# A cross-attention and FFN kernel: VectorE takes head 0's scores first, the next queries move ahead of the attention in odd heads, and the last scores get two empty banks

## The chip, the core and the metric

The kernel runs on one core of a Trainium2 chip. The metric is the device time of one launch in microseconds (us), as the median of several runs. The inputs lie in the device's memory, the output is written back to it, and nothing else is counted.

## The reference: what is computed

`x` has 8 sequences of 128 rows of 512 elements, `ctx` the same shape. The layer is a layer norm, an RMS norm, cross attention with 32 heads of width 128, a residual sum, a second layer norm and a product with a 512 x 512 matrix that is decoded from 4-bit codes (plus a low-rank term that the kernel folds into that matrix).

```python
def xattn(hidden, kv, mask, position_bias, ln_weight, w_q, w_k, w_v, w_out):
    x = rmsnorm(hidden, ln_weight)
    h_q = (x @ w_q.T).reshape(b, lq, H, DH)          # H = 32, DH = 128
    h_k = (kv @ w_k.T).reshape(b, lk, H, DH)
    h_v = (kv @ w_v.T).reshape(b, lk, H, DH)
    score = einsum('bqhd,bkhd->bhqk', h_q, h_k) + position_bias[None]
    score = softmax(where(mask, score, -inf))
    attn = einsum('bhqk,bkhd->bqhd', score, h_v).reshape(b, lq, H * DH)
    return hidden + attn @ w_out.T

x = x + xattn(layernorm(x), ctx_4096, mask, ...)
x = x + ffn(layernorm(x), w_codes, absmax, W_a, W_b)  # x @ W.T + 2 * (x @ W_a @ W_b)
```

## The kernel before

**Tiling.** All 8 sequences are taken together as 1024 columns, in two halves of 512 (`hf` 0 and 1, four sequences each). A 32-bit matmul of full precision is slow, so each operand is held as a high part (`..._hi`, rounded by ScalarE) and a low part (`..._lo`, the remainder, from VectorE or GpSimd), and `three` (L1176) issues three matmuls for each pair of tiles: high by high, low by high, high by low. `scores` (L1212) and `attend` (L1218) work on plain 32-bit tiles.

**Loops.** Heads go in groups of four (`g`), within a group `j` = 1 to 4 (head `h = 4 g + j`); head 0 is done in the prologue, and head 31 in an epilogue. Each engine has its own instruction stream, written out by hand, and the streams meet only in semaphores: `x.wait_ge(sem, n)`. So the order in each stream is the order of the calls in the source. Seven groups run in a loop, the eighth (heads 29 and 30, then 31) is written behind it.

**Keys in pairs.** The keys of two heads are made together from seven products, `key_product(m, 0..6)` of 6 matmuls each, which share three PSUM banks (w_ps0, w_ps1, w_ps2). Products 0, 2, 3 and 6 all accumulate in w_ps0. What stands there after product 0, and again after product 2, is a result of its own, and ScalarE copies it out (`copy_keys(m, n)`, L604, `kT<-w_ps`): copy 0 after product 0, copy 1 after product 1, copy 2 after product 2, copy 3 after product 6. Hence TensorE waits for copy 0 ahead of product 2 and for copy 2 ahead of product 3 (`pe.wait_ge(keys_copied, COPIES * m + 3)`).

**An odd head on TensorE** (h = 1, 3, ..., 29; `odd_head`), in this order: scores of head h; key products 0 and 1; attention of head h-1 (`attend`, which reads the probabilities pT); key product 2; the first half of the next head's queries (`queries(h + 1, 0, ...)`, 12 matmuls in a bank of its own, o_ps0); key products 3 and 4; the second half of the queries; key products 5 and 6.

**The softmax of head h.** VectorE adds the bias to the scores (L990, `p<-s_ps,p`) and takes the maxima (L992); ScalarE takes the exponentials with their sums (L653, 8 instructions) and then normalises (L604, `p_blocks<-p_blocks,row_scale`, 8 instructions), for which VectorE makes the factors (L997, L999); VectorE turns 32 x 32 blocks (L1007), and 16 DMAs of the SP queue (L341) move the blocks across partitions into pT. ScalarE's exponentials of head h+1 write p_blocks again, so they wait for these DMAs (`pT_loaded`). GpSimd writes the next head's bias into `p` (`make_bias`, L497) when the exponentials are done, splits key weights (L469, `ring_lo`), forms their sums (L459), and decodes the FFN weights in between (L532, L535).

**ScalarE in an odd head:** exponentials of the first half; copy 0; exponentials of the second half; 8 normalisations; copies 1 and 2; key weights 4, 5 and 6 (`ring_hi<-k_raw`); the two halves of the attention (`attn_hi<-s_ps`); queries (`qT<-o_ps`), weights, and so on.

**The prologue on VectorE**, behind the split of the normalised input: `residual(b)` for b = 0 to 3 (L942: `resid` scaled and shifted in place, which nothing reads before the first output sum), a context split (L893, `ctx_lo`), `residual(b)` for b = 4 to 7, the last context split (`split_first(7)`), the low part of head 1's query weights (`split_q(1)`, `q_lo`), and only then head 0's bias and maxima.

Of the kernel before, what the change touches and what calls it, by code (L numbers as in the profile page):

```python
# [7 lines left out]
B = 8  # L8
# [3 lines left out]
H = 32  # L12
# [6 lines left out]
HB = B // 2  # L19
# [42 lines left out]
SPLITS = 8  # L62
# [24 lines left out]
def key_slot(j, p):  # L87

    return (p + (PRODUCTS if j == 3 else 0)) % RING
# [6 lines left out]
def xattn_ffn(nc, x_d, ctx_d, mask_d, lnw_d, q_d, k_d, pos_d, wo_d, wv_d, codes_d, absmax_d, wa_d, wb_d, out_d):  # L96
    lora_d = nc.dram_tensor("lora_dram", (GROUPS, P, SLICE), f32, kind="Internal").ap()
    ffn_d = nc.dram_tensor("ffn_dram", (GROUPS, P, SLICE), f32, kind="Internal").ap()
    with ExitStack() as ctx:
# [107 lines left out]
            return s_ps[i][:, :, :].rearrange("p b k -> p (b k)")  # L207


        last_s = [s_ps[0][:, :, :], w_ps[2][:, :].rearrange("p (b k) -> p b k", b=HB)]  # L210

        tile_ps = [o_ps[0][:, :], o_ps[1][:, :], o_ps[2][:, :], w_ps[2][:, :]]

# [100 lines left out]
        def _(sp):  # L314
            def load_q(h):
                sp.dma_start(q_raw[:, :], q_d[h]).then_inc(q_loaded, 16)
# [50 lines left out]
            sp.wait_ge(mask_done, 2)  # L367
            load_codes(0)

            sp.wait_ge(ctx_lo_done, SPLITS)  # L370
            load_wo(0, 0)
            load_wo(1, 1)

# [8 lines left out]
            move_blocks((2, 3))  # L382
            sp.wait_ge(q_lo_done, 3)
            load_q(3)

            def group(g, last):
                for j in range(1, G if last else G + 1):
# [214 lines left out]
        def _(act):  # L602
# [167 lines left out]
            act.wait_ge(lora_stored, 16 * C)  # L770
            copy_first_values(6)
            copy_first_values(7)
            for p_at in range(2):
                split_k(1, p_at, key_slot(1, p_at))
            drain_q(1, 0, next_queries[0])
            for p_at in (2, 3):
                split_k(1, p_at, key_slot(1, p_at))
            drain_q(1, 1, next_queries[1])
            split_q(2)

            def odd_head(g, j, last):
# [109 lines left out]
        def _(dve):  # L891
# [176 lines left out]
            for b in range(HB):  # L1068
                residual(b)
            split_first(6, ctx_lo[:, 2, :, :], ctx_sum[1], ctx_hi[:, 2, :, :])  # L1070
            for b in range(HB, B):
                residual(b)
            split_first(7, ctx_lo[:, 4, :, :], ctx_sum[3], ctx_hi[:, 4, :, :])
            split_q(1)


            for hf in range(2):
                bias_and_max(0, hf)
            for hf in range(2):
                scale_rows(0, hf)  # L1080
            turn_blocks(0)
            split_q(2)

            def odd_head(g, j, last):
# [84 lines left out]
        def _(pe):  # L1169
# [149 lines left out]
            def odd_head(g, j, last):  # L1319

                h = G * g + j
                m = 2 * g + (j + 1) // 2

                pe.wait_ge(keys_added, ADDS * m)
                pe.wait_ge(attn_lo_done, 2 * (h - 1) + 2)
                scores(h, 0)

                if j == 1:
                    pe.wait_ge(values_copied, 2 * COPIES * (g + 1))
                key_product(m, 0, key_slot(j, 0))  # L1330
                key_product(m, 1, key_slot(j, 1))
                if j == 1:
                    pe.wait_ge(values_added, 2 * ADDS * (g + 1))
                pe.wait_ge(pT_loaded, 16 * NQ * NQ * h)
                for hf in range(2):
                    pe.wait_ge(biased, 2 * h + hf + 1)
                    attend(j - 1, hf, s_flat(hf), moved)
                pe.wait_ge(keys_copied, COPIES * m + 1)
                key_product(m, 2, key_slot(j, 2))

                if j == 3:
                    pe.wait_ge(out_added, B * (2 * g + 1))
                queries(h + 1, 0, query_bank(j, 0))
                pe.wait_ge(keys_copied, COPIES * m + 3)
                key_product(m, 3, key_slot(j, 3))
                key_product(m, 4, key_slot(j, 4))
                queries(h + 1, 1, query_bank(j, 1))
                key_product(m, 5, key_slot(j, 5))
                pe.wait_ge(keys_added, ADDS * m + 1)
                key_product(m, 6, key_slot(j, 6))  # L1350
# [50 lines left out]
            even_head(GROUPS - 1, 2, True)  # L1401


            pe.wait_ge(attn_lo_done, 2 * (H - 2) + 1)
            pe.wait_ge(keys_added, ADDS * PAIRS)
            scores(H - 1, 0, last_s)
            pe.wait_ge(wo_lo_done, H - 2)
            for b in range(B):
                if b % HB == 0:
                    pe.wait_ge(attn_lo_done, 2 * (H - 2) + 1 + b // HB)  # L1410
                if b in TURN_BEFORE:
# [2 lines left out]
                    for i, at in enumerate(halves(hf)):  # L1414
                        t = pe.transpose(s_ps[hf][:, i, :], p[:, at, :], ident[:, :])
                    t.then_inc(turned, 1)
                if b == 3:

                    pe.wait_ge(biased, 2 * (H - 1) + 2)
                if b >= 4:  # L1420
                    pe.wait_ge(out_added, B * (PAIRS - 2) + b - 3)
                output(b, wo_hi, wo_lo)
# [71 lines left out]
```

## Time and profile before

| | |
|---|---|
| median of 3 runs | 841.38 us (840.92 to 841.69) |
| the profiled execution's own time | 841.95 us |
| its span from the first to the last instruction | 840.1 us |
| TensorE busy | 826.6 us of the span |
| one group of four heads in the loop | 97.28 us |
| mean granted TensorE clock | 0.996 of full speed |

The execution that was profiled took 0.57 us longer than the median, and 1.85 us of its time lie outside the span. Times in rows are us from the start of the span.

### The profile page before, as it was taken

What the parts mean: (1) busy time and instruction counts of PE and PEld (TensorE: products, weight loads), DVE (VectorE), ACT (ScalarE), POOL (GpSimd) and SP (SyncE); (2) the same over time, 40 slices, a digit from 0 to 9 for tenths busy, and PEclk for the clock granted to TensorE, in tenths of its full rate; (3) what the DMA queues carried; (4) which work ended last, traced back from release to release, by engine and by line L of the source; (5) the groups of instructions that cost most, each with busy time, mean ns of one, the idle gap of its engine ahead of it and who ended that gap; (6) DMA issues with size and microseconds to landing.
All of it is one profiled execution on the core that took longest, in us unless ns stands there. A gap on an engine that the chain in (4) does not pass through costs nothing.

```text
span 840.1 us, 15757 instructions
## 1 busy us (share of the span) xinstructions
PE 826.6 (98%) x4694; PEld 721.4 (86%) x4694; DVE 450.4 (54%) x754; ACT 445.8 (53%) x1297; POOL 537.5 (64%) x556
## 2 busy tenths in 40 slices
PE   9997999999999999999999999999999999999998
PEld 6876888988889888998889888898889888898786
DVE  6783656246553556246562565436562455626683
ACT  5746555364644656264644557446553546437632
POOL 1654778756784668757786577756687567865440
PEclk9998999999999999999999999999999999999999
DMA  8213323123221223113231133112230232311102
GB/s 327 83 42 94 96 71 98 27 68 109 85 69 53 91 66 95 33 62 96 69 97 60 47 110 97 37 53 92 68 97 28 67 97 69 105 42 51 45 13 88
DMA packets 51125, 64.98 MB, mean 77 GB/s; under 512 B 11008, under 2 KB 37248, under 8 KB 50080
## 3 DMA queue, kind: packets, MB, share of 16 engines
q1 hardware_dynamic: 51104, 64.73, 24.7%
q8 instruction: 10, 0.16, 0.1%
q14 instruction: 11, 0.09, 0.0%
HBM read 44.24 MB, written 4.19 MB: 58 GB/s over the span
## 4 chain that ended last, share of the span: by engine, by line
PE 86%; DVE 5%; ACT 4%; SPq 3%; DMA 1%; issue 1%; POOL 0%; ACTq 0%; POOLq 0%; DVEq 0%
PE w_ps L1176 41%; PE o_ps L1176 32%; PE s_ps L1212 6%; PE s_ps L1218 6%; SPq L341 3%; ACT p_blocks L653 2%; ACT p_blocks L604 1%; DVE ctx_lo L893 1%; DMA pT<-p_blocks 1%; DVE stats L899 1%; DVE resid L1015 1%; DVE resid L942 1%; DVE xn_lo L948 1%; PE s_ps L1242 0%; DVE wv_raw L966 0%
## 5 line engine op out<-in xcount | busy, mean ns | idle before, releaser
L497 POOL TENSOR_TENSOR p<-pos_raw,mask_add 128x1024 f32<-128x1024 f32 x32 | 69.6, 2175 | 113.7 <-ACT p_blocks L653 113.5
L532 POOL TENSOR_SCALAR picked<-codes 128x256 f32<-128x256 int32 x112 | 125.4, 1120 | 19.2 <-POOL level L535 15.6
L653 ACT ACTIVATE p_blocks<-p,neg_max 128x128 f32<-128x128 f32 x248 | 96.1, 389 | 57.1 <-DVE neg_max L992 46.5
L535 POOL TENSOR_TENSOR level<-level,picked 128x256 f32<-128x256 f32 x112 | 89.9, 803 | 20.8 <-POOL picked L532 20.8
L469 POOL TENSOR_TENSOR ring_lo<-k_raw,ring_hi 128x256 fp32r<-128x256 f32 x105 | 76.9, 744 | 30.2 <-ACT ring_hi L604 27.2
L604 ACT ACTIVATE ring_hi<-k_raw 128x256 fp32r<-128x256 f32 x105 | 38.7, 412 | 103.3 <-POOL k_raw L459 103.3
L1015 DVE TENSOR_TENSOR resid<-o_ps,resid 128x512 f32<-128x512 f32 x102 | 68.7, 686 | 44.5 <-PE o_ps L1176 44.3
L1176 PE MATMUL w_ps<-ctx_hi,ring_hi 128*128 128x512 f32 x210 | 85.2, 406 | 0.5 <-ACT kT L604 0.5
L1176 PE MATMUL w_ps<-ctx_hi,ring_lo 128*128 128x512 f32 x210 | 82.4, 392 | 0.0
L1176 PE MATMUL w_ps<-ctx_lo,ring_hi 128*128 128x512 f32 x210 | 82.2, 392 | 0.0
L604 ACT ACTIVATE p_blocks<-p_blocks,row_scale 128x128 f32<-128x128 f32 x248 | 77.1, 390 | 1.1 <-DVE row_scale L999 1.1
L1212 PEld LDWEIGHTS s_ps<-kT,qT 128*128 128x128 f32 x504 | 62.1, 195 | 10.0 <-ACT qT L604 6.4
L1176 PE MATMUL o_ps<-wo_hi,attn_hi 128*128 128x512 f32 x180 | 70.3, 391 | 0.3 <-DVE attn_lo L893 0.3
L1212 PE MATMUL s_ps<-kT,qT 128*128 128x128 f32 x504 | 63.5, 280 | 7.1 <-ACT qT L604 7.1
L1176 PE MATMUL o_ps<-wo_hi,attn_lo 128*128 128x512 f32 x180 | 70.1, 389 | 0.0
L1176 PE MATMUL o_ps<-wo_lo,attn_hi 128*128 128x512 f32 x180 | 70.0, 389 | 0.0
L990 DVE TENSOR_TENSOR p<-s_ps,p 128x512 f32<-128x512 f32 x63 | 43.2, 686 | 40.9 <-PE s_ps L1212 40.9
L1007 DVE STREAM_TRANSPOSE p_blocks<-p_blocks 128x512 f32<-128x512 f32 x62 | 40.5, 691 | 38.0 <-ACT p_blocks L604 38.0
L1218 PEld LDWEIGHTS s_ps<-pT,v 128*128 128x128 f32 x480 | 58.2, 191 | 2.3
L1218 PE MATMUL s_ps<-pT,v 128*128 128x128 f32 x480 | 58.4, 275 | 0.0
L893 DVE TENSOR_TENSOR attn_lo<-s_ps,attn_hi 128x512 fp32r<-128x512 f32 x62 | 40.9, 680 | 31.1 <-ACT attn_hi L604 31.1
L982 DVE TENSOR_TENSOR v<-w_ps,v 128x512 f32<-128x512 f32 x21 | 14.5, 692 | 76.6 <-PE w_ps L1176 76.6
(223 smaller groups left out, 2287.9 us busy)
## 6 DMA issues: line engine op xcount, KB each, us to landing
pT<-p_blocks SPq DMA_DIRECT2D x496, 32.0 KB, 1.8
k_raw<-k_dram SPq DMA_DIRECT2D x16, 512.0 KB, 3.3
wv_raw<-wv_dram SPq DMA_DIRECT2D x8, 1024.0 KB, 4.9
q_raw<-q_dram SPq DMA_DIRECT2D x32, 256.0 KB, 3.5
wo_raw<-wo_dram SPq DMA_DIRECT2D x32, 256.0 KB, 3.9
resid<-x_dram SPq DMA_DIRECT2D x2, 1024.0 KB, 12.0
pos_raw<-pos_dram SPq DMA_DIRECT2D x32, 64.0 KB, 3.9
out_dram<-resid SPq DMA_DIRECT2D x8, 256.0 KB, 2.0
```

The costliest lines, as they stand in the source:

```text
L469: return pool.tensor_tensor(out, whole, hi.bitcast(f32), ALU.subtract)
L497: pool.tensor_tensor(p[:, :, :], pos, mask_add[:, :, :], ALU.add).then_inc(bias_done, 1)
L532: then(pool.tensor_scalar((level if code == 0 else picked)[:, :], codes[:, :], float(code), NF4[code], match, ALU.mult))
L535: then(pool.tensor_tensor(level[:, :], level[:, :], picked[:, :], ALU.add))
L604: return act.activation(out, in_, ACT.Copy, **kw)
L653: e = act.activation(out(b), p[:, b, :].rearrange("p (k c) -> p k c", c=Q), ACT.Exp, bias=neg_max[:, b:b + 1], accum_out=prob_sum[:, b:b + 1])
L893: return dve.tensor_tensor(out, whole, hi.bitcast(f32), ALU.subtract)
L990: dve.tensor_tensor(p[:, bs, :], banks[hf][:, :, :], p[:, bs, :], ALU.add).then_inc(biased, 1)
L1015: dve.tensor_tensor(resid[:, b, :], bank, resid[:, b, :], ALU.add).then_inc(out_added, 1)
L1176: mm = pe.matmul(out, l, r, start=opens and i == 0, stop=closes and i == n - 1, skip_group_check=True)
L1212: s = pe.matmul(banks[hf][:, i, :], qT[:, at], kT[:, slot, at], start=True, stop=True)
L1218: o = pe.matmul(out[:, i * L:(i + 1) * L], v[:, b, j * DH:(j + 1) * DH], by_keys(b), start=True, stop=True)
```

## The change

It has four parts, and no instruction is added or taken away.

1. VectorE's prologue: head 0's bias and maxima stand right behind the split of context part 6. `split_q(1)` follows, then the factors of half 0, `residual(4)`, the factors of half 1, `residual(5)` to `residual(7)`, the turn of the blocks, and last `split_first(7)`. SP waits for five context splits, no longer for all eight, ahead of its first output-weight loads; the wait for all eight stands further down.
2. ScalarE's prologue: the copies of head 1's queries (`drain_q(1, 0)`, `drain_q(1, 1)`) stand behind the first and the second key weight split, no longer behind the second and the fourth.
3. TensorE's odd heads: `queries(h + 1, 0, ...)` stands behind key product 1, ahead of the attention, no longer between key products 2 and 3. Its wait for the output sums moves with it.
4. The epilogue: the scores of head 31 go to the banks o_ps2 and w_ps2, no longer s_ps0 and w_ps2; the wait for the attention's low part goes, and output 2 waits for the first half's bias sum.

```diff
-        last_s = [s_ps[0][:, :, :], w_ps[2][:, :].rearrange("p (b k) -> p b k", b=HB)]
+        last_s = [bank[:, :].rearrange("p (b k) -> p b k", b=HB) for bank in (o_ps[2], w_ps[2])]
@@ sync
-            sp.wait_ge(ctx_lo_done, SPLITS)
+            sp.wait_ge(ctx_lo_done, 5)
             load_wo(0, 0)
             load_wo(1, 1)
...
             load_q(3)
+
+            sp.wait_ge(ctx_lo_done, SPLITS)
@@ scalar
-            for p_at in range(2):
-                split_k(1, p_at, key_slot(1, p_at))
+            split_k(1, 0, key_slot(1, 0))
             drain_q(1, 0, next_queries[0])
+            split_k(1, 1, key_slot(1, 1))
+            drain_q(1, 1, next_queries[1])
             for p_at in (2, 3):
                 split_k(1, p_at, key_slot(1, p_at))
-            drain_q(1, 1, next_queries[1])
             split_q(2)
@@ vector
             split_first(6, ctx_lo[:, 2, :, :], ctx_sum[1], ctx_hi[:, 2, :, :])
-            for b in range(HB, B):
-                residual(b)
-            split_first(7, ctx_lo[:, 4, :, :], ctx_sum[3], ctx_hi[:, 4, :, :])
-            split_q(1)
             for hf in range(2):
                 bias_and_max(0, hf)
-            for hf in range(2):
-                scale_rows(0, hf)
+            split_q(1)
+            scale_rows(0, 0)
+            residual(HB)
+            scale_rows(0, 1)
+            for b in range(HB + 1, B):
+                residual(b)
             turn_blocks(0)
+            split_first(7, ctx_lo[:, 4, :, :], ctx_sum[3], ctx_hi[:, 4, :, :])
             split_q(2)
@@ tensor, odd_head
                 key_product(m, 1, key_slot(j, 1))
                 if j == 1:
                     pe.wait_ge(values_added, 2 * ADDS * (g + 1))
+                else:
+                    pe.wait_ge(out_added, B * (2 * g + 1))
+                queries(h + 1, 0, query_bank(j, 0))
                 pe.wait_ge(pT_loaded, 16 * NQ * NQ * h)
                 for hf in range(2):
                     pe.wait_ge(biased, 2 * h + hf + 1)
                     attend(j - 1, hf, s_flat(hf), moved)
                 pe.wait_ge(keys_copied, COPIES * m + 1)
                 key_product(m, 2, key_slot(j, 2))
-
-                if j == 3:
-                    pe.wait_ge(out_added, B * (2 * g + 1))
-                queries(h + 1, 0, query_bank(j, 0))
                 pe.wait_ge(keys_copied, COPIES * m + 3)
                 key_product(m, 3, key_slot(j, 3))
@@ tensor, epilogue
-            pe.wait_ge(attn_lo_done, 2 * (H - 2) + 1)
             pe.wait_ge(keys_added, ADDS * PAIRS)
             scores(H - 1, 0, last_s)
...
-                if b == 3:
-                    pe.wait_ge(biased, 2 * (H - 1) + 2)
+                if b in (2, 3):
+                    pe.wait_ge(biased, 2 * (H - 1) + b - 1)
```

TensorE's stream in an odd head of the loop, from the attention (`s_ps<-pT,v`) on, before. The six `w_ps<-ctx...` rows are key product 2, `o_ps<-xn_hi,q_hi` is the first matmul of the next queries, and ISA and REGISTER_ALU rows carry waits and counters.

```order
L1218 MATMUL s_ps<-pT,v 128x128 x8
L1338 ISA
L1182 REGISTER_ALU
L1176 MATMUL w_ps<-ctx_hi,ring_hi 128x512
L1176 MATMUL w_ps<-ctx_lo,ring_hi 128x512
L1176 MATMUL w_ps<-ctx_hi,ring_lo 128x512
L1176 MATMUL w_ps<-ctx_hi,ring_hi 128x512
L1176 MATMUL w_ps<-ctx_lo,ring_hi 128x512
L1176 MATMUL w_ps<-ctx_hi,ring_lo 128x512
L1202 REGISTER_ALU
L1176 MATMUL o_ps<-xn_hi,q_hi 128x512
```

The same place in the change, again from the attention on:

```order
L1221 MATMUL s_ps<-pT,v 128x128 x8
L1345 ISA
L1185 REGISTER_ALU
L1179 MATMUL w_ps<-ctx_hi,ring_hi 128x512
L1179 MATMUL w_ps<-ctx_lo,ring_hi 128x512
L1179 MATMUL w_ps<-ctx_hi,ring_lo 128x512
L1179 MATMUL w_ps<-ctx_hi,ring_hi 128x512
L1179 MATMUL w_ps<-ctx_lo,ring_hi 128x512
L1179 MATMUL w_ps<-ctx_hi,ring_lo 128x512
L1347 REGISTER_ALU
L1185 REGISTER_ALU
L1179 MATMUL w_ps<-ctx_hi,ring_hi 128x512
```

The queries stood behind key product 2; now L1347, the wait for the copy, and key product 3 stand right behind it.

VectorE's stream in the prologue before, from context split 6 on (`p<-s_ps,p` and `neg_max` are head 0's bias and maxima, `recip` and `row_scale` its factors):

```order
L893 TENSOR_TENSOR ctx_lo<-wv_raw,ctx_hi 128x1024
L942 TENSOR_SCALAR resid<-resid,ln_scale,ln_shift 128x512 x4
L893 TENSOR_TENSOR ctx_lo<-wv_raw,ctx_hi 128x1024
L893 TENSOR_TENSOR q_lo<-q_raw,q_hi 128x512
L990 TENSOR_TENSOR p<-s_ps,p 128x512
L992 TENSOR_REDUCE neg_max<-p 128x4
L990 TENSOR_TENSOR p<-s_ps,p 128x512
L992 TENSOR_REDUCE neg_max<-p 128x4
L997 RECIPROCAL recip<-prob_sum 128x4
L999 TENSOR_TENSOR row_scale<-recip,row_valid 128x4
L997 RECIPROCAL recip<-prob_sum 128x4
L999 TENSOR_TENSOR row_scale<-recip,row_valid 128x4
```

And in the change, from the same split on:

```order
L895 TENSOR_TENSOR ctx_lo<-wv_raw,ctx_hi 128x1024
L992 TENSOR_TENSOR p<-s_ps,p 128x512
L994 TENSOR_REDUCE neg_max<-p 128x4
L992 TENSOR_TENSOR p<-s_ps,p 128x512
L994 TENSOR_REDUCE neg_max<-p 128x4
L895 TENSOR_TENSOR q_lo<-q_raw,q_hi 128x512
L999 RECIPROCAL recip<-prob_sum 128x4
L1001 TENSOR_TENSOR row_scale<-recip,row_valid 128x4
L944 TENSOR_SCALAR resid<-resid,ln_scale,ln_shift 128x512
L999 RECIPROCAL recip<-prob_sum 128x4
L1001 TENSOR_TENSOR row_scale<-recip,row_valid 128x4
L944 TENSOR_SCALAR resid<-resid,ln_scale,ln_shift 128x512 x3
```

Four residuals and one context split stood ahead of the bias sum. Now one residual stands between the factors and three stand between the last factor and the turn of the blocks.

## Rows read from the trace of the kernel before

**Rows 1.** The page, part 1: busy us (share of span) xinstructions.

```profile
PE 826.6 (98%) x4694; PEld 721.4 (86%) x4694; DVE 450.4 (54%) x754; ACT 445.8 (53%) x1297; POOL 537.5 (64%) x556
```

**Rows 2.** TensorE's waits: us in total, times, longest us.

```profile
PE s_ps L1212 <- ACT qT L604: 7.1, 3, 4.8
...
PE w_ps L1176 <- ACT kT L604: 0.5, 1, 0.5
```

**Rows 3.** Stretch of one group: us, then busy us of each engine, clock, DMA.

```profile
245.33:342.61 97.28, 97.28 (x574) 86.25 (x573) 49.62 (x84) 51.58 (x157) 67.69 (x69) 1.00 0.24 73
```

**Rows 4.** Timeline of TensorE in odd head 13: start us, us, instruction.

```profile
368.52 1.95 PE L1218 MATMUL s_ps<-pT,v 128*128 128x128 f32 x16
370.22 0.48 PE L1176 MATMUL w_ps<-ctx_hi,ring_hi 128*128 128x512 f32 x1
...
371.46 0.39 PE L1176 MATMUL w_ps<-ctx_hi,ring_lo 128*128 128x512 f32 x1
371.69 0.40 PE L1176 MATMUL o_ps<-xn_hi,q_hi 128*128 128x512 f32 x1
...
374.43 0.39 PE L1176 MATMUL w_ps<-ctx_hi,ring_hi 128*128 128x512 f32 x1
...
379.64 0.39 PE L1176 MATMUL o_ps<-xn_hi,q_lo 128*128 128x512 f32 x1
```

**Rows 5.** Timeline of ScalarE in the same head.

```profile
372.59 1.06 ACT L604 ACTIVATE kT<-w_ps 128x512 f32<-128x512 f32 x2
373.55 1.02 ACT L604 ACTIVATE ring_hi<-k_raw 128x256 fp32r<-128x256 f32 x3
...
380.07 0.60 ACT L604 ACTIVATE qT<-o_ps 128x512 f32<-128x512 f32 x1 [3.01 <-PE o_ps L1176]
```

**Rows 6.** Timeline of GpSimd in the same head.

```profile
374.13 2.14 POOL L469 TENSOR_TENSOR ring_lo<-k_raw,ring_hi 128x256 fp32r<-128x256 f32 x3 [1.29 <-ACT ring_hi L604]
```

**Rows 7.** Timeline of TensorE, head 0's scores to head 1.

```profile
49.03 2.01 PE L1212 MATMUL s_ps<-kT,qT 128*128 128x128 f32 x16
...
66.71 1.88 PE L1212 MATMUL s_ps<-kT,qT 128*128 128x128 f32 x8 [4.76 <-ACT qT L604]
...
81.87 0.49 PE L1176 MATMUL w_ps<-ctx_hi,ring_hi 128*128 128x512 f32 x1 [0.48 <-ACT kT L604]
```

**Rows 8.** Timeline of VectorE in the prologue.

```profile
46.02 2.58 DVE L942 TENSOR_SCALAR resid<-resid,ln_scale,ln_shift 128x512 f32<-128x512 f32 x4
...
49.66 3.13 DVE L942 TENSOR_SCALAR resid<-resid,ln_scale,ln_shift 128x512 f32<-128x512 f32 x4
...
54.45 0.68 DVE L990 TENSOR_TENSOR p<-s_ps,p 128x512 f32<-128x512 f32 x1
...
59.33 2.00 DVE L999 TENSOR_TENSOR row_scale<-recip,row_valid 128x4 f32<-128x4 f32 x1
62.67 1.30 DVE L1007 STREAM_TRANSPOSE p_blocks<-p_blocks 128x512 f32<-128x512 f32 x2 [1.34 <-ACT p_blocks L604]
```

**Rows 9.** Timeline of ScalarE: head 0's normalisation, head 1's exponentials, copies 1 and 2.

```profile
58.99 1.27 ACT L604 ACTIVATE p_blocks<-p_blocks,row_scale 128x128 f32<-128x128 f32 x4
...
74.76 0.40 ACT L653 ACTIVATE p_blocks<-p,neg_max 128x128 f32<-128x128 f32 x1 [4.79 <-DMA pT<-p_blocks]
...
80.68 1.05 ACT L604 ACTIVATE kT<-w_ps 128x512 f32<-128x512 f32 x2
```

**Rows 10.** Timelines of GpSimd and of SP's queue: head 1's bias, head 0's moves.

```profile
59.16 2.15 POOL L497 TENSOR_TENSOR p<-pos_raw,mask_add 128x1024 f32<-128x1024 f32 x1 [6.65 <-ACT p_blocks L653]
...
63.41 10.08 SPq L341 DMA_DIRECT2D pT<-p_blocks  x16
```

**Rows 11.** Timelines of ScalarE and TensorE ahead of head 31's scores.

```profile
781.60 1.06 ACT L604 ACTIVATE qT<-w_ps 128x512 f32<-128x512 f32 x2
...
782.32 1.13 PE L1212 MATMUL s_ps<-kT,qT 128*128 128x128 f32 x8 [1.37 <-ACT qT L604]
```

**Rows 12.** Stretch behind TensorE's long pause, columns as in rows 3.

```profile
67.00:71.00 4.00, 3.07 (x15) 2.78 (x15) 0.99 (x2) 1.72 (x4) 3.02 (x5) 0.50 0.20 52
```

## The prediction

> **What bounds the kernel now.** I read the busy times first: TensorE is busy for 826.6 of 840.1 us [rows 1], so only what TensorE has to do or wait for can count. Next comes the table of its waits: 7.1 us for ScalarE's copies of queries, in three waits, and a single wait of 0.5 us for a copy of keys [rows 2]; all but the last of the three query waits lie in the first 80 us. Then a stretch of one whole group: 97.28 us, TensorE busy for all of it [rows 3]. So the loop has no wait of TensorE's that a new order could take away, and any wait that a new order puts in is paid in full. What can be won lies in the prologue, at the pause of 4.76 us ahead of head 1's scores [rows 7], and ahead of head 31's scores, where TensorE waits 1.37 us [rows 11].
>
> **The odd heads, part 3 of the change.** In head 13 key product 2 issues its last matmul at 371.46; 12 matmuls of queries follow from 371.69, and key product 3 starts at 374.43 [rows 4]. Product 3 must wait until ScalarE has copied product 2 out of the bank. That copy is the second of the pair at 372.59, which ends at 373.65 [rows 5], 0.8 us before product 3 is due. The cover is exactly the queries, 374.43 - 371.69 = 2.74 us, and the change takes them away: now product 3 is the next instruction behind product 2.
>
> What is exposed is worked out so. From the start of the last matmul of a product to the start of ScalarE's copy it is 380.07 - 379.64 = 0.43 us [rows 4, 5], if ScalarE is free. The copy takes 0.60 [rows 5]. From the end of such a copy to TensorE's next matmul it is 0.14: the pair of copies from 80.68 ends at 81.73, and TensorE starts at 81.87 [rows 7, 9]. That makes 1.17 us from matmul to matmul, where the cadence is 371.69 - 371.46 = 0.23 [rows 4]: 0.94 lost. The first matmul behind such a wait takes 0.49 instead of 0.39 [rows 7]: 0.10 more. Together 1.04 us. The lower bound leaves out the 0.14 and the 0.10 (the next matmul may be ready to go the moment that the copy ends): 0.80. The upper bound is 1.15, for a slower run-in over several matmuls (product 2 itself spends 371.46 - 370.22 = 1.24 us on five intervals behind the attention, 0.1 over cadence [rows 4]).
>
> Is ScalarE free then? In the change the attention is 2.74 us later, so product 2 runs where the queries ended and its last matmul starts near 374.2. ScalarE has done copy 1 by 373.1 [rows 5] and is idle from there. Yes. Who stands behind copy 2 on ScalarE: key weights 4 to 6, which started at 373.55 [rows 5] and now start near 375.1; GpSimd takes them 0.58 later [rows 5, 6] and each needs 0.71 [rows 6], so part 4 is ready at 376.4, and product 4 wants it near 376.8, some 0.4 us to spare. Behind that come the attention's copies and VectorE's sums, 1.6 us later than now, with idle time of 3.01 us on ScalarE in front of the second query copy to absorb it [rows 5]. SP's moves of pT wait for the attention of the head before, which ends near 373.2; the turned blocks are ready about when they were. I cost all this at nothing; if the 0.4 us were gone, product 4 would wait too (a rival below).
>
> How often? There are 15 odd heads, 1 to 29. Head 1 has its exponentials late already and waits for the same copies as now, so its wait belongs to the prologue. Head 29 is special: behind it the chain through SP's moves and ScalarE releases head 31's scores at 782.32, 1.37 us after TensorE is ready [rows 11]. A delay of TensorE's by 1.04 us there disappears in that wait. The second query copy becomes due near 782.1, later than now, but the eight score matmuls of the first half cover it. I take -0.1 for this place. Heads 3 to 27 are 13: 13 x 1.04 = **+13.5 us** (10.4 to 15.0). Nothing gives it back, since the loop has no other TensorE wait [rows 2, 3].
>
> **The prologue, parts 1 and 2.** Head 0's scores start at 49.03; the first half is written at about 50.1 (half of 2.01 us [rows 7]). VectorE now takes them at 54.45 [rows 8], behind four residuals (3.13 us from 49.66 [rows 8]), a split and `q_lo`. Without these it can start near 50.2, 4.2 us sooner, and the exponentials end near 54.8 instead of 59.0 [rows 9]. `split_q(1)` behind the maxima ends near 53.6; TensorE's second query block for it starts at 56.3, so it hides.
>
> The next link is a collision. The factor instruction at 59.33 takes 2.00 us, beside GpSimd's bias from 59.16 to 61.31 [rows 8, 10]. Both are released by the same exponential, so I expect it again, 4.2 us earlier, over at 57.2; the second half is normalised by 58.4. But VectorE has three residuals ahead of the turn now: 3 x 0.65 (2.58 us for four [rows 8]), so the turn starts at 59.1 instead of 62.67 [rows 8]: **-3.5 us**. The Trainium skill, page "SBUF — State Buffer", section "SBUF: two separate sides", says that VectorE with two SBUF inputs and GpSimd take a port pair as an exclusive lock, the loser standing still for the other's whole instruction; the trace agrees (2.00 us for 4 elements a row). Were there no collision this time, the turn could start at 57.4, 5.2 us sooner. Were the residuals slow, at 0.78 each [rows 8], it would be 3.1. These are the bounds: 3.1 to 5.2.
>
> From the turn on, distances stay: SP issues 16 moves from 63.41 for 10.08 us [rows 10], the exponentials of head 1 start 12.09 us after the turn (74.76 - 62.67 [rows 8, 9]), and product 3 of head 1 starts 7.11 us after those (81.87 - 74.76 [rows 7, 9]). So product 3 starts at 78.4 instead of 81.87. The pause of 4.76 us ahead of the scores goes, by part 2: the first query copy comes near 60, the second near 62.3. TensorE then waits later: about 1.8 us for pT ahead of the attention, 0.5 ahead of product 2, and about 3.4 ahead of product 3, where the moved queries no longer fill the time. What the two halves of the prologue give is therefore the chain's 3.5 us, not the pause.
>
> **The epilogue, part 4.** What head 31's scores wait for is the query copy [rows 11], not the bank. Zero; the earlier wait for the bias at output 2 comes 2.7 us behind the scores and VectorE is ready by then.
>
> **Sum.** -3.5 + 13.5 - 0.1 = +9.9 us on the profiled execution's 841.95, that is 851.9; that execution is 0.6 over the median, so against 841.38 it gives **851.3 us**.
>
> **Rivals.**
>
> *The clock falls in the pause ahead of product 3 of head 1 (25 in 100).* After the pause of 4.76 us the granted clock is 0.50 (1.2 GHz) from 67 to 71 [rows 12]; after the 1.37 us ahead of head 31's scores eight score matmuls still take 1.13 us against 1.88 behind the long pause [rows 7, 11]. The new 3.4 us lies between. If it falls, some 3.3 us of matmuls take twice as long as they should, an estimate from rows 12's stretch of 4 us at half speed: +1.6, so 852.9. The Trainium skill, page "TensorE: Matmul & The Clock Gate", section "Why this matters for your kernels", warns that one idle gap in the middle of a kernel sends the clock back to half; that is this rival.
>
> *A second wait at product 4 (8 in 100).* If GpSimd's part 4 comes 0.3 us too late in each head, beyond its 0.4 us to spare: 13 x 0.3 = +3.9, so 855.2.
>
> *The prologue gives nothing (4 in 100).* The turn isn't earlier because the residuals and the collision add up: 851.3 + 3.5 = 854.8.
>
> *Faster (5 in 100).* The wait for copy 2 stays covered. For it: in a matmul row the end is modelled, and ScalarE might be released before the 0.39 us are over. Against it: 0.43 us from start to copy is read from ScalarE's own start. If it were covered in full, 841.4 - 3.6 = 837.8 us; the point from which it decides is 3.6 / 13 = 0.28 us per head, a third of the lower bound. Within 0.2% (1.7 us, about what a measurement of this kernel can tell from no change) would be 0.15 to 0.4 us per head: 3 in 100.
>
> *My forecast (55 in 100).*
>
> **How the numbers follow.** The likeliest case alone: 841.4 - 5.2 + 10.4 - 0.3 = 846.3 at the lowest, 841.4 - 3.1 + 15.0 = 853.3 at the highest. With the clock's rival its top goes to 854.9. Extremes of both terms at once are unlikely, so the range for 8 in 10 is 847.0 to 854.5. Slower by over 0.2%: 92 in 100; within: 3; faster: 5.
>
> **What the profile after would show.** TensorE's wait table has `w_ps L1176 <- ACT kT` some 14 or 15 times, 0.8 to 1.0 us each, and a group takes 99.4 us instead of 97.28; head 1's first scores follow the queries without the 4.76 us; the turn of head 0's blocks starts near 59 and the moves of pT near 60. I am wrong if the group stays at 97.3 us (the copy is covered), if it is over 100 us (a second wait), or if head 1's product 3 doesn't start within a microsecond of 78.4.

## The result and the profile after

The change makes the kernel slower: 851.25 us (850.97 to 851.89) against 841.54 us (840.92 to 842.23) for the kernel before on the same chip, a ratio of 1.0116 with a 95% interval of 1.0099 to 1.0134. The forecast was 851.3. The profiled execution took 851.89 us, 9.94 us over the profiled execution of before (841.95); its span is 850.1 us against 840.1.

The page's part 1 of the kernel after (busy us, share, instructions; answers to [rows 1]):

```profile
PE 829.5 (98%) x4694; PEld 719.7 (85%) x4694; DVE 455.3 (54%) x754; ACT 447.9 (53%) x1297; POOL 539.0 (63%) x556
```

TensorE's waits after (us in total, times, longest; answers to [rows 2]):

```profile
PE w_ps L1179 <- ACT kT L606: 14.0, 16, 3.2
...
PE s_ps L1221 <- DMA pT<-p_blocks: 0.5, 1, 0.5
...
PE s_ps L1215 <- ACT qT L606: 0.4, 1, 0.4
```

The 7.1 us of waits for query copies have shrunk to two of 0.4, and the wait for copies of keys has grown from one to sixteen. Of those, two belong to head 1, and 14 to the odd heads from 3 on: 0.76 us each, 0.69 in head 29.

Stretch of one group after (us, then busy us of PE, PEld, DVE, ACT and POOL, clock, DMA; answers to [rows 3]):

```profile
266.33:365.65 99.32, 97.80 (x574) 86.09 (x573) 50.86 (x84) 51.83 (x157) 68.00 (x68) 1.00 0.23 72
```

A group takes 99.32 us where it took 97.28. TensorE's busy time is nearly the same (97.80); 1.52 us are now idle, two waits of 0.76. The group holds two odd heads, so each costs 2.04 / 2 = 1.02 us: the wait and a slower start behind it.

TensorE in odd head 13 after (start us, us; answers to [rows 4]):

```profile
374.63 0.48 PE L1179 MATMUL w_ps<-ctx_hi,ring_hi 128*128 128x512 f32 x1
...
375.87 0.40 PE L1179 MATMUL w_ps<-ctx_hi,ring_lo 128*128 128x512 f32 x1
377.03 0.51 PE L1179 MATMUL w_ps<-ctx_hi,ring_hi 128*128 128x512 f32 x1 [0.76 <-ACT kT L606]
377.38 0.39 PE L1179 MATMUL w_ps<-ctx_lo,ring_hi 128*128 128x512 f32 x1
```

And ScalarE there (answers to [rows 5]):

```profile
376.30 0.60 ACT L606 ACTIVATE kT<-w_ps 128x512 f32<-128x512 f32 x1 [1.42 <-PE w_ps L1179]
376.80 1.02 ACT L606 ACTIVATE ring_hi<-k_raw 128x256 fp32r<-128x256 f32 x3
```

The round trip can be read off step by step: last matmul of product 2 at 375.87, copy at 376.30 (0.43 later), 0.60 of copy, product 3 at 377.03 (0.13 later). ScalarE had been idle for 1.42 us, so nothing but TensorE's own result was late. Product 3's second matmul starts 0.35 behind the first, 0.12 more than the cadence of 0.23.

TensorE in the prologue after (answers to [rows 7]):

```profile
48.90 2.01 PE L1215 MATMUL s_ps<-kT,qT 128*128 128x128 f32 x16
...
61.67 1.05 PE L1215 MATMUL s_ps<-kT,qT 128*128 128x128 f32 x8
...
63.14 1.16 PE L1215 MATMUL s_ps<-kT,qT 128*128 128x128 f32 x8 [0.42 <-ACT qT L606]
...
70.32 2.05 PE L1221 MATMUL s_ps<-pT,v 128*128 128x128 f32 x16 [0.55 <-DMA pT<-p_blocks]
...
77.42 0.50 PE L1179 MATMUL w_ps<-ctx_hi,ring_hi 128*128 128x512 f32 x1 [3.20 <-ACT kT L606]
...
79.06 0.63 PE L1179 MATMUL w_ps<-ctx_hi,ring_hi 128*128 128x512 f32 x1
```

The pause of 4.76 us ahead of head 1's scores is gone; 3.20 us of waiting stand ahead of product 3, and 1.6 us behind that wait the matmuls lengthen from 0.39 to 0.63 us.

VectorE in the prologue after (answers to [rows 8]):

```profile
49.99 0.69 DVE L992 TENSOR_TENSOR p<-s_ps,p 128x512 f32<-128x512 f32 x1 [1.35 <-PE s_ps L1215]
...
54.88 1.99 DVE L1001 TENSOR_TENSOR row_scale<-recip,row_valid 128x4 f32<-128x4 f32 x1
56.80 1.45 DVE L944 TENSOR_SCALAR resid<-resid,ln_scale,ln_shift 128x512 f32<-128x512 f32 x3
58.23 1.30 DVE L1009 STREAM_TRANSPOSE p_blocks<-p_blocks 128x512 f32<-128x512 f32 x2
```

GpSimd's bias starts at 54.71 and takes 2.14, so the factors collide with it as before (1.99 us for what takes 0.17 alone). Behind them the three residuals take 0.48 us each.

Head 31's scores after (answers to [rows 11]):

```profile
792.25 1.13 PE L1215 MATMUL o_ps<-kT,qT 128*128 128x128 f32 x8 [0.44 <-ACT qT L606]
```

And the stretch behind product 3's wait (columns as in the stretch of one group; answers to [rows 12]), with a granted clock of 0.59:

```profile
78.00:82.00 4.00, 4.00 (x12) 3.14 (x11) 1.93 (x4) 2.69 (x6) 3.71 (x5) 0.59 0.19 49
```

**Where the 9.96 us are.** I take the start of each head's scores in both traces, and the difference after minus before. This table is worked out from the two timelines.

| piece of the trace | before | after | difference |
|---|---|---|---|
| start of head 0's scores | 49.03 | 48.90 | -0.13 |
| from there to product 3 of head 1 | 32.84 | 28.52 | -4.32 |
| from product 3 to head 2's scores | 8.30 | 9.91 | +1.61 |
| from head 2's scores to head 3's | 20.54 | 19.95 | -0.59 |
| head 3's scores to head 28's (13 odd heads) | 602.27 | 615.59 | +13.32 |
| head 28's to head 31's scores | 69.34 | 69.38 | +0.04 |
| head 31's scores to the last matmul | 54.22 | 54.25 | +0.03 |

### The profile page after: what moved, and what is told of

It reads as the page before. It is cut to its first block, busy times and chain, and to the rows that moved or that the text cites. A ratio compares the mean times of both kernels' runs of the same rounds, so it can differ in the third digit from the quotient of the medians.

```text
span 850.1 us, 15758 instructions
## 1 busy us (share of the span) xinstructions
PE 829.5 (98%) x4694; PEld 719.7 (85%) x4694; DVE 455.3 (54%) x754; ACT 447.9 (53%) x1297; POOL 539.0 (63%) x556
## 4 chain that ended last, share of the span: by engine, by line
PE 92%; ACT 3%; DVE 3%; SPq 1%; issue 1%; DMA 0%; POOL 0%; ACTq 0%; POOLq 0%
PE w_ps L1179 44%; PE o_ps L1179 33%; PE s_ps L1215 6%; PE s_ps L1221 6%; ACT kT L606 1%; ACT p_blocks L655 1%; SPq L341 1%; DVE stats L901 1%; DVE resid L1017 1%; PE s_ps L1179 1%; ACT p_blocks L606 0%; PE s_ps L1245 0%; PE o_ps L1245 0%; PE w_ps L1281 0%; PE w_ps L1236 0%
## 5 line engine op out<-in xcount | busy, mean ns | idle before, releaser
L534 POOL TENSOR_SCALAR picked<-codes 128x256 f32<-128x256 int32 x112 | 128.8, 1150 | 19.2 <-POOL level L537 15.6
L537 POOL TENSOR_TENSOR level<-level,picked 128x256 f32<-128x256 f32 x112 | 87.4, 781 | 20.8 <-POOL picked L534 20.8
L1179 PEld LDWEIGHTS w_ps<-ctx_hi,ring_hi 128*128 128x128 f32 x210 | 39.7, 189 | 27.2 <-issue 19.4
L1215 PEld LDWEIGHTS s_ps<-kT,qT 128*128 128x128 f32 x496 | 59.8, 191 | 2.5 <-ACT qT L606 0.6
L1215 PE MATMUL s_ps<-kT,qT 128*128 128x128 f32 x496 | 60.7, 275 | 0.4 <-ACT qT L606 0.4
L606 ACT ACTIVATE kT<-w_ps 128x512 f32<-128x512 f32 x63 | 37.1, 591 | 42.2 <-PE w_ps L1179 42.2
```

What stands on the lines that cost most here:

```text
L534: then(pool.tensor_scalar((level if code == 0 else picked)[:, :], codes[:, :], float(code), NF4[code], match, ALU.mult))
L537: then(pool.tensor_tensor(level[:, :], level[:, :], picked[:, :], ALU.add))
L606: return act.activation(out, in_, ACT.Copy, **kw)
L1179: mm = pe.matmul(out, l, r, start=opens and i == 0, stop=closes and i == n - 1, skip_group_check=True)
L1215: s = pe.matmul(banks[hf][:, i, :], qT[:, at], kT[:, slot, at], start=True, stop=True)
```

## The experiments

Each kernel is the changed one with one edit, if not said otherwise. Each was timed in turn with the kernel before, whose median was 841.21 us beside e1 to e4, 840.72 beside e5b, e6, e7 and e7b, 840.77 beside e8 and e9, and 840.95 beside e10 and e11. A ratio is to that median, with its 95% interval. The start of the program differs by up to 2.15 us between the profiled executions (head 0's scores start between 47.98 and 50.13), so stretches of the prologue are measured from head 0's scores. Each trace is one execution. The mean granted clock of all the others is on record too, and it shows that the clock falls in some executions of a kernel and not in others, as said under e6.

### e1 and e2: part 3 undone, and part 3 alone

The edit of e1; e2 makes the opposite edit on the kernel before.

```diff
-                queries(h + 1, 0, query_bank(j, 0))
                 pe.wait_ge(pT_loaded, 16 * NQ * NQ * h)
                 ...
                 key_product(m, 2, key_slot(j, 2))
+                queries(h + 1, 0, query_bank(j, 0))
```

> The change with its part 3 undone: the first query block stands behind key product 2 again. Theory of the copy wait: in the changed kernel each of heads 3 to 27 loses 1.02 us ahead of product 3, 13.3 us in all; all of it comes back, a group takes 97.3 us again, and the gain of the prologue is left: 837.1 us if the TensorE clock stays up in head 1, 838.1 if it falls as it does in the change. Rival: the loss comes from another part of the change (the scores' order, the last banks, the port shared with GpSimd): then this stays near 850.

> The kernel before with part 3 alone. Theory of the copy wait: 841.5 + 13 x 1.02 = 854.8 us, with head 1 unchanged (its product 3 waits for the same late copy as before) and head 29 absorbed by the wait ahead of head 31's scores. Rival, that the moved queries fill a pause in head 1 and give something there: 852 to 853.

e1: 837.64 us (836.36 to 838.40), ratio 0.996 (0.9946 to 0.9973). e2: 854.66 us (853.71 to 857.34), ratio 1.0162 (1.0148 to 1.0176). Part 3 costs 13.6 us on the other parts (851.25 - 837.64) and 13.4 on the kernel before (854.66 - 841.21), so it adds up with the rest. Both came out as the theory of the copy wait said. TensorE's waits in e2:

```profile
PE w_ps L1176 <- ACT kT L604: 11.4, 15, 0.8
PE s_ps L1212 <- ACT qT L604: 5.9, 3, 4.8
```

The fifteen waits of 0.8 come, and the long query wait stays, since parts 1 and 2 aren't there. In e2 each odd head loses 1.02 us (from head 3's scores to head 28's the trace falls 13.26 us behind), in e1 none does: 0.00.

In e1 the long pause moves instead to the attention, and the clock falls behind it:

```profile
70.77 3.78 PE L1221 MATMUL s_ps<-pT,v 128*128 128x128 f32 x16 [3.29 <-DMA pT<-p_blocks]
```

The attention takes 3.78 us instead of 2.05.

### e3 and e4: how much cover the copy needs

The twelve query matmuls are divided: some ahead of the attention, the rest behind product 2, three in e3 and six in e4. A helper `queries_part` issues them by chunks of three (a range of `c`).

```diff
-                queries(h + 1, 0, query_bank(j, 0))
+                queries_part(h + 1, 0, query_bank(j, 0), 0, 2)    # e3: 0, 3
                 ...
                 key_product(m, 2, key_slot(j, 2))
+                queries_part(h + 1, 0, query_bank(j, 0), 2, C)    # e3: 3, C
```

> The change with the query block cut: 9 of its 12 matmuls ahead of the attention, 3 behind key product 2. Theory of the copy wait: 3 x 0.227 = 0.68 us of the 0.93 are covered, 0.25 plus the slow first matmul (0.12) are left, 0.37 per head: 841.5 - 3.4 + 13 x 0.37 = 842.9 us. Rival, a loss in proportion to what was moved ahead (9 of 12): 841.5 - 3.4 + 0.75 x 13.3 = 848.1.

> As before, cut in the middle: 6 matmuls ahead of the attention and 6 behind key product 2. Theory of the copy wait: 6 x 0.227 = 1.36 us cover the 0.93 in full, so no wait is left in the loop: 838.1 us, or 837.1 if the shorter pause in head 1 keeps the clock up. Rival, in proportion (6 of 12): 841.5 - 3.4 + 6.7 = 844.8.

e3: 842.27 us (841.50 to 843.43), ratio 1.0017 (1.0008 to 1.0026). e4: 837.16 us (836.42 to 838.11), ratio 0.996 (0.9947 to 0.9974). TensorE in head 13 of e3, behind product 2's last matmul at 371.71:

```profile
371.71 0.39 PE L1179 MATMUL w_ps<-ctx_hi,ring_lo 128*128 128x512 f32 x1
371.94 0.40 PE L1179 MATMUL o_ps<-xn_hi,q_hi 128*128 128x512 f32 x1
...
372.41 0.40 PE L1179 MATMUL o_ps<-xn_hi,q_lo 128*128 128x512 f32 x1
372.87 0.49 PE L1179 MATMUL w_ps<-ctx_hi,ring_hi 128*128 128x512 f32 x1
```

Product 3 starts 372.87 - 371.71 = 1.16 us behind product 2's last matmul, exactly as in the change: the round trip is fixed, and three matmuls fill 0.69 of it. What is left is small enough that the profile hardly shows it as a wait, yet each odd head loses 0.354 us (4.60 us over 13). With six matmuls (1.4 us) nothing is lost. So the loss per head is 1.02, 0.35 and 0.00 us for a cover of 0, 3 and 6 matmuls. A loss in proportion to what was moved ahead would have given 848.1 and 844.8 us.

### e5b, e8 and e9: what the turn of head 0's blocks waits for

e5b is e4 with GpSimd's first bias released later, by the second factor instead of by the exponentials:

```diff
-            pool.wait_ge(exp_done, 2)
+            pool.wait_ge(row_scale_done, 2)
             make_bias(1)
```

e9 is e4 with the last three residuals behind the turn and the last context split; e8 has both edits:

```diff
             scale_rows(0, 1)
-            for b in range(HB + 1, B):
-                residual(b)
             turn_blocks(0)
             split_first(7, ctx_lo[:, 4, :, :], ctx_sum[3], ctx_hi[:, 4, :, :])
+            for b in range(HB + 1, B):
+                residual(b)
```

> The kernel cut in the middle (6 and 6), and GpSimd's bias for head 1 released by the second row factors instead of by the exponentials, so that it can't hold the instruction that makes them. Theory of the collision: the factors take 0.16 us instead of 1.99, ScalarE normalises the second half at once, the turn of head 0's blocks starts near 57.1 instead of 58.2, and the whole chain to head 1's product 3 with it: 837.2 - 1.1 = 836.1 us. Rival, that the three residuals beside the bias are slowed in its place and hold the turn: 836.8 to 837.2.

> Cut in the middle, GpSimd's bias behind the second row factors, and the last three residuals behind the turn and the last context split. Theory: the residuals were what held the turn once the bias came later (3.28 us for three beside it, where they take 1.45 alone); without them the turn follows ScalarE's normalisation, 1.2 us sooner than in the kernel with the bias alone moved, and the chain to head 1's product 3 with it: 835.7 us. Rival, that head 1 is by now held by something that doesn't hang on the turn (the scores, or a context split that is late): 836.6 to 837.2.

> Cut in the middle and the last three residuals behind the turn, the bias where it was. Theory: the factors are held by the bias for 1.99 us again, so ScalarE's normalisation ends when it did and the turn can't be earlier: 837.2 us, as with the cut alone. Rival, that the residuals alone held the turn: 835.7 to 836.2.

| kernel | us | ratio (95%) | turn | product 3 | head 2's scores |
|---|---|---|---|---|---|
| e4 | 837.16 | 0.996 (0.9947 to 0.9974) | 9.32 | 28.52 | 36.83 |
| e5b | 836.81 (836.28 to 837.35) | 0.9949 (0.9935 to 0.9962) | 9.26 | 28.43 | 36.73 |
| e9 | 837.29 (836.03 to 838.63) | 0.9959 (0.9945 to 0.9972) | 9.32 | 28.50 | 38.39 |
| e8 | 836.55 (835.49 to 838.03) | 0.995 (0.9936 to 0.9963) | 8.11 | 27.29 | 37.21 |

The last three columns are us from the start of head 0's scores. VectorE in e5b:

```profile
54.54 0.16 DVE L1001 TENSOR_TENSOR row_scale<-recip,row_valid 128x4 f32<-128x4 f32 x1
54.62 3.28 DVE L944 TENSOR_SCALAR resid<-resid,ln_scale,ln_shift 128x512 f32<-128x512 f32 x3
57.83 1.29 DVE L1009 STREAM_TRANSPOSE p_blocks<-p_blocks 128x512 f32<-128x512 f32 x2
```

The factor is free of the collision (0.16 us), but the residuals now lie beside the bias (GpSimd, 54.78 to 57.16) and take 1.09 us each instead of 0.48. Nothing is won: 1.83 us less for the factor, 1.83 more for the residuals. Taking only the residuals away (e9) wins nothing either, because the second half's normalisation, released by the slow factor, ends as late. So e9 came out as expected and e5b as its rival had it (836.1 expected). Both together (e8) bring the turn 1.2 us forward. VectorE in e8:

```profile
55.03 0.16 DVE L1001 TENSOR_TENSOR row_scale<-recip,row_valid 128x4 f32<-128x4 f32 x1
57.16 1.30 DVE L1009 STREAM_TRANSPOSE p_blocks<-p_blocks 128x512 f32<-128x512 f32 x2 [1.97 <-ACT p_blocks L606]
```

The turn came forward as expected, but the time of e8 missed its 835.7 us by 0.9, and its trace keeps next to nothing of the 1.2: head 2's scores come at 37.21 against 36.83, and head 3's at 57.17 against 57.29. In this trace the clock is low at another place. TensorE in e4:

```profile
70.00 2.73 PE L1229 MATMUL s_ps<-pT,v 128*128 128x128 f32 x16 [1.91 <-DMA pT<-p_blocks]
...
77.08 0.49 PE L1179 MATMUL w_ps<-ctx_hi,ring_hi 128*128 128x512 f32 x1 [0.66 <-ACT kT L606]
```

and in e8:

```profile
76.34 0.49 PE L1179 MATMUL w_ps<-ctx_hi,ring_hi 128*128 128x512 f32 x1 [1.81 <-ACT kT L606]
```

The stretch behind this wait in e8, where the granted clock is 0.68:

```profile
78.00:82.00 4.00, 4.00 (x14) 3.15 (x13) 2.47 (x5) 1.62 (x4) 3.54 (x5) 0.68 0.19 49
```

In e4 the clock is low during the attention, and product 3 waits afterwards for ScalarE anyway (0.66 us are left of that wait): the slow matmuls are free. In e8 it is low behind product 3, where TensorE waits for nothing up to head 2's scores, and pays. But this is what the two profiled executions did, and not shown to be the work of the edits: of e8's five executions three have a mean granted clock of 1.000 (835.49 to 836.55 us) and two a lower one (836.96, which was profiled, and 838.03).

### e6, e7 and e7b: parts 4 and 2 undone

e6 gives the last scores their old banks and waits; e7 puts ScalarE's query copies back behind the second and the fourth key weight split; e7b does so on e1, so that only parts 1 and 4 remain.

```diff
             split_k(1, 0, key_slot(1, 0))
-            drain_q(1, 0, next_queries[0])
             split_k(1, 1, key_slot(1, 1))
-            drain_q(1, 1, next_queries[1])
+            drain_q(1, 0, next_queries[0])
             for p_at in (2, 3):
                 split_k(1, p_at, key_slot(1, p_at))
+            drain_q(1, 1, next_queries[1])
```

> The change with its part 4 undone (head 31's scores in s_ps0 again, with the wait for the attention's low part). Theory: the scores wait for the query copy, not for the bank, so nothing changes: 851.3 us. Rival, that the bank's release would be late once the query copy comes earlier or the attention is late: 851.8 or more, with a wait of TensorE's for VectorE's attn_lo in the row of head 31's scores.

> The change with its part 2 undone (ScalarE copies head 1's queries behind the second and the fourth key weight split). Theory of the chain: product 3 of head 1 is released by the turn, the moves and the exponentials, so later scores only eat into TensorE's pause of 3.2 us: 851.3 us, at most 1 us off it either way by where the clock falls. Rival, that the pause of 4.76 us ahead of the scores was what the prologue lost: 853 or more.

> Parts 1 and 4 alone: queries behind product 2, query copies in their old place. Theory of the chain: as with part 2, 837.6 us, at most 1 us off either way by where the clock falls. Rival, as in the kernel above: 839.5 or more.

e6: 851.50 us (850.97 to 851.83), ratio 1.0124 (1.0109 to 1.0140), no change against 851.25: part 4 is worth nothing, and head 31's scores still wait for the query copy, 0.42 us.

e6 also shows something of the clock. Its prologue is the change's, instruction for instruction, and TensorE waits there as it does in the change. Yet behind the same wait ahead of product 3 its granted clock is 1.00, where the change had 0.59:

```profile
77.89 0.49 PE L1179 MATMUL w_ps<-ctx_hi,ring_hi 128*128 128x512 f32 x1 [3.19 <-ACT kT L606]
...
78.00:82.00 4.00, 4.00 (x18) 3.29 (x19) 2.94 (x6) 3.17 (x8) 3.49 (x5) 1.00 0.17 43
```

So whether the clock falls there is a matter of the execution: the order and the waits of the kernel don't settle it. The mean granted clock says the same: 0.998 in three executions of the change and 1.000 in the fourth, 1.000 in two of e6 and 0.998 in two. The two traces price the fall: from product 3 of head 1 to head 3's scores it is 29.86 us in the change and 28.59 in e6, 1.27 less. The times hardly show it (850.97 at 1.000 against 851.20 to 851.89 in the change), since their spread is as large.

e7: 850.19 us (849.97 to 851.71), ratio 1.0106 (1.0091 to 1.0122). e7b: 836.86 us (835.91 to 837.51), ratio 0.995 (0.9936 to 0.9963), against 837.64 in e1. Neither rival came (853 or more, 839.5 or more). The intervals overlap, so part 2 is not shown to be worth or to cost anything; e7's median is one of executions with the clock at 1.000 (849.97 to 850.29), that of the change one with a fall. The profiled execution of e7 is the fourth (851.71, mean granted clock 0.996): behind waits of 1.31 and 1.64 us for the query copies its clock is 0.50 from 66 to 70, and product 3 comes 30.30 us from head 0's scores instead of 28.52, though head 3's scores come at 58.52, hardly later than in the change (58.38).

```profile
65.76 2.08 PE L1215 MATMUL s_ps<-kT,qT 128*128 128x128 f32 x8 [1.64 <-ACT qT L606]
...
66.00:70.00 4.00, 4.00 (x14) 3.52 (x15) 3.58 (x5) 0.22 (x1) 1.85 (x2) 0.50 0.20 51
```

With the old copies the same waiting is spread over the prologue. TensorE in e7b, whose stream up to there is the same and whose clock stays up:

```profile
62.31 1.16 PE L1215 MATMUL s_ps<-kT,qT 128*128 128x128 f32 x8 [1.31 <-ACT qT L606]
...
65.11 1.16 PE L1215 MATMUL s_ps<-kT,qT 128*128 128x128 f32 x8 [1.64 <-ACT qT L606]
...
69.52 2.05 PE L1221 MATMUL s_ps<-pT,v 128*128 128x128 f32 x16 [0.49 <-DMA pT<-p_blocks]
...
76.60 0.49 PE L1179 MATMUL w_ps<-ctx_hi,ring_hi 128*128 128x512 f32 x1 [0.48 <-ACT kT L606]
```

Every matmul there runs at full speed, and the granted clock is 1.00 from 66 to 82 us. Product 3 comes at 28.51 us from head 0's scores, no later than in the change (28.52).

### e10 and e11: the versions that follow

e10 has the queries back (as e1), the old copies, the later bias and the later residuals. e11 is e8 with the old copies, so it keeps six query matmuls ahead of the attention.

> Parts 1 and 4 alone (queries behind product 2, query copies in their old place), with the bias behind the second row factors and the last three residuals behind the turn. Theory: the turn comes 1.2 us sooner, and TensorE's pauses in head 1 are short enough in this order that the clock stays at 1.00, as it did with parts 1 and 4 alone: 836.9 - 1.2 = 835.7 us. Rival, that TensorE's own work in head 1 is the longer path by now, or that the clock falls: 836.5 to 837.3.

> The same with the query block cut in the middle (6 ahead of the attention, 6 behind product 2). Theory: the same turn; TensorE has 6 matmuls less to do behind the attention, which is worth nothing if product 3 waits for ScalarE: 835.7 us. Rival, a fallen clock ahead of or behind product 3: 836.5 to 837.3.

e10: 836.28 us (834.35 to 837.77), ratio 0.9946 (0.9932 to 0.9959), 0.6 over the 835.7 that was expected. e11: 835.54 us (835.40 to 836.57), ratio 0.9937 (0.9924 to 0.9951), as expected. Both reach product 3 at 27.3 us and head 2's scores at 35.6, 1.2 us ahead of e4, with the clock at 1.00 from 70 to 82 us in both traces (among all executions two of e10 and one of e11 have a mean below 1.000). TensorE in e11:

```profile
64.17 1.16 PE L1223 MATMUL s_ps<-kT,qT 128*128 128x128 f32 x8 [1.83 <-ACT qT L606]
...
69.27 1.95 PE L1229 MATMUL s_ps<-pT,v 128*128 128x128 f32 x16
...
75.47 0.49 PE L1179 MATMUL w_ps<-ctx_hi,ring_hi 128*128 128x512 f32 x1 [1.48 <-ACT kT L606]
```

These two are faster than both kernels. e11 has the lowest median of all, 5.4 us under the kernel before, but its interval overlaps with those of every version that has the loop's cover back (e10, e5b, e8, e7b, e9, e4, e1), so none of these is shown to be faster than another.

## Why the prediction was right, point by point

**The odd heads.** This term carries the result and its mechanism is shown. The step "1.17 us from matmul to matmul" measured 1.16, in the change and again in e3; the run-in taken as 0.10 measured 0.12; per head 1.04 was forecast and 1.02 measured, 13.5 against 13.32 over the 13 heads. Undoing the move removes it (e1), the move alone brings it (e2), and it falls with the cover as the fixed round trip says (e3, e4). The covered-copy rival is ruled out.

**Who stands behind copy 2.** GpSimd starts the key weights at 377.38, 0.58 behind ScalarE as before, and no product 4 waits. That rival had nothing.

**Heads 29 and 31.** The delay of 0.98 us in head 29 was taken back all but 0.04 at head 31's scores, whose wait fell from 1.37 to 0.44 us: +0.04 in the table, where I had taken -0.1. The lowest sum has -0.3 there, which no row gives; it moves that bound by 0.2 us.

**The prologue.** The total is right, -3.43 us against -3.5 (with the start, up to head 3's scores), but that is luck: its parts missed and cancelled.

- "3 x 0.65" for the residuals ahead of the turn was mis-sized. They took 1.45 us together, 0.48 each: I had taken the mean of four residuals elsewhere. That is 0.5 of the 0.9 us by which the turn came sooner (58.23 instead of 59.1); the rest was there before the residuals, since the factors were done at 56.8 instead of 57.2. Product 3 came at 77.42 instead of 78.4, just inside the microsecond I had allowed. The collision itself came as forecast (1.99 us).
- The clock's rival, at 25 in 100, did occur in the profiled execution, and by the mean granted clock in two of the other three. Its slow stretch has the size I gave: product 3 to head 2's scores takes 9.91 us instead of 8.30, +1.6. But 0.59 of it came back within head 2 against the kernel before, which I had not foreseen, and 0.33 against e6 (19.95 instead of 20.28). In e6 ScalarE's exponentials of head 2 wait 2.78 us for head 1's moves of pT, which a faster TensorE doesn't bring forward; in the change they are released by VectorE's maxima. How much comes back depends on that chain: in e10, with the clock at 1.00 and pT sooner, product 3 to head 3's scores takes 28.26 us, in e6 28.59, in e4, the kernel before and e7b 28.77, 28.84 and 28.98, and 29.86, 29.88 and 29.84 in the change, e8 and e9, whose clock falls behind product 3. So the net price of the fall is 1.27 us by the like pair, and between 0.9 and 1.6 by the others. That head 1's moves set what comes back is read from these waits, not tested.

With the residuals as slow as I took them the change would have taken 0.5 us more, 851.8, an estimate from these terms; without the clock's fall the traces would make it 1.3 us less, 850.0, while the one execution without it took 850.97. All lie in the range; the point forecast was closer than its parts.

**Smaller pauses.** I had 1.8 us ahead of the attention, 0.5 ahead of product 2 and 3.4 ahead of product 3; the trace has 0.55, 0.19 and 3.20. The first fell short in the main since pT came 0.9 us sooner with the turn.

**What the parts are worth.** Parts 1 and 4 alone give 836.86 (e7b), 3.9 us under the 840.72 of the kernel before timed beside it, and since part 4 is worth nothing, all of it is part 1's (whether VectorE's order alone does it, without SP's earlier output-weight loads, was not tested). The way from the turn to product 3 is 19.20 us before and 19.19 in the change, so what the turn gains arrives whole. This bears out that the chain through the turn counts and not the pause it shortens: part 2 removes the largest wait in TensorE's table and wins nothing that the times show, because product 3 is released by the turn, the moves and the exponentials, whenever the scores come. The change as a whole loses because part 3 gives 13.5 us back.

**Open.** Why the clock falls in one execution of the same prologue and not in the next, and which of the versions from e1 to e11 is truly the fastest.

## What to carry to other kernels

Matmuls that stand between a product and the next one in the same bank are cover for the copy: before moving them, add up the copy's round trip and leave as many as it needs (here 1.16 us, which by the cadence of 0.23 us five matmuls of 512 columns should fill, an estimate; six were enough, three were not). A loss of a microsecond in a loop without slack is paid in every pass, and thirteen of them outweighed all that this prologue won. When a later wait is released by a chain that doesn't hang on the earlier one, removing the earlier only lengthens the later. And before a microsecond is put down to an edit, compare two traces of the same stretch: here the clock alone moved 1.27 us between executions of the same instructions.

## What the runs showed of the hardware

- **The round trip.** TensorE's last matmul of 512 columns to ScalarE's copy is 0.43 us, the copy of a 128x512 bank 0.60, back to TensorE 0.13, and the first interval behind the wait 0.35 instead of 0.23.
- **Residuals beside GpSimd.** The same VectorE instruction (128x512, scaled and shifted in place by two factors) took 0.48 us each in the change with GpSimd idle (56.85 to 59.64), 1.09 beside the bias in e5b, and 0.93 in e8 beside GpSimd's key weights and sums. So not only the factors with two inputs in SBUF take longer beside GpSimd. That GpSimd is the cause is read from the overlap in time, and from the bias that was moved away from the factor (0.16 instead of 1.99).
- **The clock.** It was 0.50 behind pauses of 4.76 us (before) and 3.29 (e1), and low in the stretches behind 3.20 (after, 0.59), 2.47 (e5b, 0.65), 1.91 (e4, 0.66 from 70 to 75), 1.81 (e8, 0.68), 1.83 (e9, 0.63) and 1.64 (e7, 0.50). It stayed at 1.00 behind 3.19 in e6, 1.83 and 1.48 in e11, and 1.31 and 1.64 in e7b. The change and e6, and e7 and e7b, have the same stream and the same waits up to there, so in these cases neither the length of a pause nor the kernel's pattern of pauses settles it. The kernel before, with its 4.76 us, has a mean below 1.000 in each of 39 executions (0.993 to 0.996). The Trainium skill, page "TensorE: Matmul & The Clock Gate", section "Why this matters for your kernels", warns of a single idle gap between matmuls, if it is long enough, as what sends the clock back. The traces agree that the clock falls behind gaps, and not that the length of one gap decides. What a fall costs depends on its place: 1.27 us net behind product 3 (the change against e6), and nothing that shows in e4, where product 3 comes at the same 28.52 us, ahead of a wait that would have come anyway.
